# Four-head attention: the target row of a batch's first source tile added by a TensorE identity product instead of by VectorE

## The chip, the core and the metric

One NeuronCore of one Trainium2 chip runs the whole program; the other cores are idle. The metric is the device time of one execution in microseconds. The core has five engines that work through their own instruction lists in order and wait for each other on semaphores: TensorE (PE in the profile; its weight loads are PEld), VectorE (DVE), ScalarE (ACT), GpSimd (POOL) and SyncE (SP), which here issues DMAs.

## The reference, cut to what matters

The program is a four-layer graph network over 3125 nodes with 256 features. The change touches one of its stages, the first attention of the last layer, with HEADS = 4 and HID = 64:

```python
h = (x @ W).reshape(n, heads, ch)
es = (h * a_src).sum(-1)
ed = (h * a_dst).sum(-1)
e = jax.nn.leaky_relu(es[src] + ed[dst], 0.2)
m = jax.ops.segment_max(e, dst, num_segments=n)
w = jnp.exp(e - m[dst])
den = jax.ops.segment_sum(w, dst, num_segments=n)
alpha = w / den[dst]
out = jax.ops.segment_sum(h[src] * alpha[:, :, None], dst, num_segments=n)
```

The kernel computes it densely: for every head, every source node s and every target node t it forms the weight exp(leaky_relu(es[s] + ed[t]) - m[t]), multiplies it by the number of edges from s to t, and sums over the sources with matmuls.

## The kernel before

The stage is `dense_attention(K, "att2", given, 4, LOOPED, ...)`. The 3125 nodes are 25 tiles of 125 (`NPT`). A round `r` is one head `h = r // 5` and one group `g = r % 5` of five target tiles (`GW` = 625 targets in the free dimension); there are 20 rounds. A round has five batches (`q` = 0 to 4) of five source tiles (`UN` = 5), so there are 100 batches `b`. A batch lives in one of four ring slots, `ring[:, b % RB]`, as 125 source partitions x 5 tiles x 625 targets in fp32. The leaky ReLU is split: with `src8` = 0.8 es, `src2` = 0.2 es and `dst8` = 0.8 ed, the exponent is relu(src8 + dst8[t]) + low[t] + src2, where low[t] = 0.2 ed[t] - m[t]. The rows dst8 and low, the same in all 128 partitions, are `rows[:, r % 2, 0, :]` and `rows[:, r % 2, 1, :]` (the target row).

Each batch passes through these steps, each an instruction list's part on its engine:

- ACT `bend(b)` (L2009): five Relu activations of the dst8 row with bias src8 into the ring, semaphore `s_z`. It is issued two batches ahead, and waits for TensorE to have finished batch b-4 of the slot.
- DVE `lower(b)` (L1915): one tensor_tensor of 3125 columns adds the target row to all five tiles, semaphore `s_w` (in batch 0, five instructions of one tile).
- ACT exps (L2051): five Exp activations with bias src2, in place, semaphore `s_e`; they wait for `s_w`.
- DVE `weigh(b)` (L1934): min with 1 and times the edge counts `cell`, 3125 columns, semaphore `s_p`; it waits for all five exps.
- PE, for each of the five tiles, two accumulating matmuls (L2113 with 500 and L2115 with 125 columns; each shows as two instructions, since fp32 takes two passes) into PSUM banks 0 and 1 or 2 and 3, semaphore `s_mm`.

DVE's order is `lower(b+1)`, `weigh(b)`, then as a rule one `look` (L1875, 3125 columns of masks, the maximum for a coming round; the 100 looks are done by batch 92), and in q = 2 also `shift` (L1885 to L1890, five-column steps). ACT's order in batch b is: exps of b; in q = 3 `rows_out(r+1)` (L1990, L1991: the new rows from PSUM banks 5, 6 and 7); in q = 1 of the groups 1, 2 and 3 of the first three heads `row_out` (L1997: up to three copies of the next head's source scores, out of banks 5, 6 and 7); `bend(b+2)`; in q = 1 `evict(r-1)` (L2020, L2022: the finished sums to SBUF); in q = 2 `settle(r-1)` (L2034, L2035). PE's order in batch b is: the matmuls of b; in q = 0 `turn_back(r-1)` (L2095, waits for `evict`); in q = 2 `spread(r+1)` (L2078, 20 instructions that write banks 5, 6 and 7, after `shift`); in q = 4 of the first three groups of the first three heads `row` (L2085, up to 24 instructions that write banks 5, 6 and 7). SP loads the cells and masks into three buffers each. In the last head DVE also does `finish` in q = 3 (L1942 to L1948).

The same function with one head (att1 and att3, `fused`) has other steps, which the change leaves as they are.

Of the kernel before, what the change touches and what calls it, by code (L numbers as in the profile page):

```python
# [6 lines left out]
ALU = mybir.AluOpType  # L7
ACT = mybir.ActivationFunctionType
# [8 lines left out]
P = 128  # L17
# [3 lines left out]
NPT = 125  # L21
# [10 lines left out]
UN = 5  # L32
GW = UN * NPT
# [1757 lines left out]
def dense_attention(K, tag, given, heads, loops, bias_name, relu=False, to_aux=False):  # L1791
# [4 lines left out]
    f, NG5 = D // heads, NT // UN  # L1796
    NGR = heads * NG5
# [6 lines left out]
    MM, OUTS = (2, 2) if across else (UN, 2 * UN)  # L1804

# [4 lines left out]
    with Phase(nc, tag) as ph:  # L1810
# [6 lines left out]
        if across:  # L1817
            s_turned, s_back, turned = ph.sem("turned"), ph.sem("back"), ph.sb("turned", [P, GW])
        rows = ph.sb("rows", [P, 2, 2, GW])
# [46 lines left out]
        def _(dve):  # L1866
# [26 lines left out]
            def lower(b):  # L1893
# [3 lines left out]
                parts = UN if b == 0 else 1  # L1897
# [13 lines left out]
                for i in range(0 if fused else parts):  # L1911
                    n = UN // parts
                    dve.wait_ge(s_z, b * UN + (i + 1) * n)
                    here = ring[0:NPT, b % RB, i * n:(i + 1) * n, :]
                    dve.tensor_tensor(here, here, rows[0:NPT, r % 2, 1, :].unsqueeze(1).to_broadcast([NPT, n, GW]),  # L1915
                                      ALU.add).then_inc(s_w, n)
# [39 lines left out]

            dve.tensor_scalar(dst8[0:NPT, :, 0:heads], K.score_dst[0:NPT, :, 0:heads], 0.8, None, ALU.mult).then_inc(s_parts, 1)
# [25 lines left out]
        def _(act):  # L1983

            def rows_out(r):

                act.wait_ge(s_wide, r + 1)
                if r >= 2:
                    act.wait_ge(s_w, (r - 1) * UN * UN)
                act.copy(rows[:, r % 2, :, 0:BAND], K.ps[:, 5:7, 0:BAND]).then_inc(s_rows, 1)  # L1990
                act.copy(rows[:, r % 2, :, BAND:GW], K.ps[:, 7, 0:2 * NPT].rearrange("p (j n) -> p j n", j=2)).then_inc(s_rows, 1)  # L1991
# [7 lines left out]
            def bend(b):  # L1999

                r = b // UN
                h = r // NG5
                if b % UN == 0:
                    act.wait_ge(s_rows, (r + 1) * 2)
                for u in range(UN):
                    s = b % UN * UN + u
                    if b >= RB:
                        act.wait_ge(s_mm, ((b - RB) * UN + u + 1) * MM)
                    act.activation(ring[0:NPT, b % RB, u, :], rows[0:NPT, r % 2, 0, :], ACT.Relu,  # L2009
                                   bias=src8[0:NPT, s, h:h + 1]).then_inc(s_z, 1)  # L2010
# [34 lines left out]
            for b in range(NB):  # L2045
                r, q = b // UN, b % UN
                h, g = r // NG5, r % NG5
                for u in range(UN):
                    act.wait_ge(s_w, b * UN + (u + 1 if fused or b == 0 else UN))
                    here = ring[0:NPT, b % RB, u, :]  # L2050
                    act.activation(here, here, ACT.Exp, bias=src2[0:NPT, q * UN + u, h:h + 1]).then_inc(s_e, 1)  # L2051
                if q == 3 and r + 1 < NGR:
                    rows_out(r + 1)
                if q == 1 and g in (1, 2, 3) and h + 1 < heads:
                    for j in range(3 if g < 3 else 1):
                        row_out(h + 1, (g - 1) * 3 + j, 5 + j)
# [11 lines left out]
        def _(pe):  # L2068
# [28 lines left out]

            for i in range(7):
                row(0, i, i)
            pe.wait_ge(s_rowed, 7)  # L2100
            pe.wait_ge(s_parts, 3)
            spread(0)
            for b in range(NB):
                r, q = b // UN, b % UN
                h, g = r // NG5, r % NG5
                for v in range(UN):
# [18 lines left out]
                if q == 2 and r + 1 < NGR:  # L2125
                    spread(r + 1)
                if q == 4 and g < 3 and h + 1 < heads:
                    pe.wait_ge(s_rows, (r + 2) * 2)
                    for j in range(3 if g < 2 else 1):
                        row(h + 1, g * 3 + j, 5 + j)  # L2130
# [970 lines left out]
```

## Time and profile before

| what | value |
|---|---|
| median of 3 runs | 6654.85 us (6648.68 to 6659.43) |
| profiled execution, its own time | 6659.23 us |
| span of the profile | 6657.5 us |
| granted TensorE clock, mean over the span | 0.896 |
| four-head attention in the profile | from 4942.8 to 6018 us |

All times are microseconds unless ns is written. DVE, ACT and PE are busy when an instruction of theirs runs. An idle time in square brackets is that before the instruction, with what released it. The granted clock is a share of 2.4 GHz; it has the two levels 2.4 and 1.2 GHz.

### The profile page before, as it was taken

What the parts mean: (1) busy time and instruction counts of PE and PEld (TensorE: products, weight loads), DVE (VectorE), ACT (ScalarE), POOL (GpSimd) and SP (SyncE); (2) the same over time, 40 slices, a digit from 0 to 9 for tenths busy, and PEclk for the clock granted to TensorE, in tenths of its full rate; (3) what the DMA queues carried; (4) which work ended last, traced back from release to release, by engine and by line L of the source; (5) the groups of instructions that cost most, each with busy time, mean ns of one, the idle gap of its engine ahead of it and who ended that gap; (6) DMA issues with size and microseconds to landing.
All of it is one profiled execution on the core that took longest, in us unless ns stands there. A gap on an engine that the chain in (4) does not pass through costs nothing. (4 is left out here: it accounts for less than half of the span.)

```text
span 6657.5 us, 73453 instructions
## 1 busy us (share of the span) xinstructions
PE 4892.2 (73%) x21195; PEld 3419.5 (51%) x21196; DVE 4365.2 (66%) x7225; ACT 2060.1 (31%) x3736; POOL 1498.1 (23%) x1522
## 2 busy tenths in 40 slices
PE   0110888877888899999697789399927777776989
PEld 0000444433444677788585658378823333334877
DVE  9991999858999433423794370301049999997956
ACT  0000111131111233322332233122227777773432
POOL 4776666515666000011000010200020000000010
PEclk9995899978999899999898989599968888887989
DMA  3330333473334200044330012256534444433310
GB/s 96 139 128 24 102 100 101 93 305 114 113 100 98 44 9 15 7 114 118 117 115 28 2 47 75 93 181 183 166 96 157 153 156 153 155 127 98 127 33 20
DMA packets 376014, 682.91 MB, mean 103 GB/s; under 512 B 90858, under 2 KB 302883, under 8 KB 368132
## 3 DMA queue, kind: packets, MB, share of 16 engines
q1 hardware_dynamic: 300148, 522.74, 24.0%
q0 software_dynamic: 75344, 157.40, 9.2%
q8 instruction: 87, 1.43, 0.1%
q14 instruction: 115, 0.94, 0.0%
q10 hardware_dynamic: 320, 0.40, 0.0%
HBM read 507.64 MB, written 172.62 MB: 102 GB/s over the span
## 5 line engine op out<-in xcount | busy, mean ns | idle before, releaser
L896 PE MATMUL ps<-sum_hot_cell,sum_hot_src 128*128 128x500 bf16 x2640 | 762.1, 391 | 363.9 <-DVE sum_hot_src L835 221.2
L813 POOL DMA_INDIRECT sum_rows_in<-rel_table,rel_row x880 | 835.0, 949 | 471.5 <-issue 235.6
L837 DVE TENSOR_SCALAR sum_hot_cell<-x_nodes 128x1500 bf16<-128x1500 f16 (+1 forms) x880 | 892.0, 1014 | 2.2 <-issue 2.2
L2113 PE MATMUL ps<-att_ring,acc 125*65 125x500 f32 x1000 | 603.0, 689 | 306.8 <-DVE att_ring L1934 306.8
L2051 ACT ACTIVATE att_ring<-att_ring,att_src 125x625 f32<-125x625 f32 x750 | 555.8, 808 | 257.1 <-DVE att_ring L1909 158.1
L902 PE MATMUL ps<-sum_rows_in,sum_hot 128*128 128x256 f32 x1760 | 582.2, 411 | 50.0 <-issue 48.2
L896 PEld LDWEIGHTS ps<-sum_hot_cell,sum_hot_src 128*128 128x128 bf16 x2640 | 265.2, 101 | 668.8 <-issue 480.8
L2121 PE MATMUL ps<-acc,att_ring 125*125 125x257 f32 x2500 | 556.1, 385 | 45.9 <-DVE att_ring L1934 45.9
L2121 PEld LDWEIGHTS ps<-acc,att_ring 125*125 125x125 f32 x2500 | 474.6, 190 | 124.6 <-DVE att_ring L1934 50.3
L1875 DVE CUSTOM_DVE_ANT_0 att_held<-att_held,aux 125x3125 bf16<-125x3125 bf16 x150 | 510.3, 3408 | 33.2 <-ACT aux L1997 21.1
L1934 DVE SCALAR_TENSOR_TENSOR att_ring<-att_ring,att_held 125x3125 f32<-125x3125 f32 (+1 forms) x162 | 511.7, 3165 | 1.6 <-ACT att_ring L2051 1.3
L669 POOL DMA_INDIRECT rec_dram<-rec,addr x392 | 429.4, 1095 | 124.0 <-issue 124.0
L902 PEld LDWEIGHTS ps<-sum_rows_in,sum_hot 128*128 128x128 f32 x1760 | 314.2, 199 | 183.9 <-issue 91.1
L857 ACT COPY acc<-ps 128x256 f32<-128x256 f32 x50 | 18.6, 372 | 1143.5 <-PE ps L902 790.3
L2744 POOL TENSOR_TENSOR x_nodes<-x_nodes,aux 128x256 f32<-128x256 f32 x25 | 20.3, 852 | 1561.0 <-POOLq L118 1561.0
L833 DVE TENSOR_SCALAR sum_hot<-row_f,slot_dst,slot_w 128x128 f32<-128x128 f32 x880 | 308.6, 351 | 93.3 <-remote 47.9
L2009 ACT ACTIVATE att_ring<-att_rows,att_src 125x625 f32<-125x625 f32 x500 | 363.3, 803 | 0.6
L1915 DVE TENSOR_TENSOR att_ring<-att_ring,att_rows 125x3125 f32<-125x3125 f32 (+1 forms) x104 | 341.2, 3284 | 12.0 <-ACT att_ring L2009 11.9
L2115 PEld LDWEIGHTS ps<-att_ring,acc 125*65 125x65 f32 x1000 | 155.8, 156 | 353.4 <-issue 353.4
L1662 DVE TENSOR_TENSOR experts_y<-ps,expert_bo 128x256 f32<-128x256 f32 x200 | 84.9, 424 | 362.1 <-PE ps L1729 362.1
L1048 PE MATMUL ps<-aux,sum_wide 125*125 125x256 f32 x1250 | 298.5, 386 | 14.0 <-ACT sum_wide L986 14.0
L2113 PEld LDWEIGHTS ps<-att_ring,acc 125*65 125x65 f32 x1000 | 137.1, 158 | 326.3 <-DVE att_ring L1934 326.3
(471 smaller groups left out, 8347.5 us busy)
## 6 DMA issues: line engine op xcount, KB each, us to landing
att_held<-cells SPq DMA_DIRECT2D x150, 781.2 KB, 4.7
att_held<-masks SPq DMA_DIRECT2D x150, 762.9 KB
rel_table<-rel_stage SPq DMA_DIRECT2D x50, 2048.0 KB, 6.5
ffn_w<-in_L_ffn_W SPq DMA_DIRECT2D x64, 1024.0 KB, 7.6
sum_cell<-cells SPq DMA_DIRECT2D x125, 156.2 KB, 4.6
sage_cell<-cells SPq DMA_DIRECT2D x125, 156.2 KB, 2.2
masks<-att_held POOLq DMA_DIRECT2D x25, 762.9 KB, 11.8
sum_rows_in<-rel_table,rel_row POOLq DMA_INDIRECT x880
```

The source lines that it names most:

```text
L669: pool.indirect_dma_start(K.rec_dram, bass.IndirectOffsetOnAxis(addr[:, j:j + 1], 0), rec[:, j, :], None).then_inc(scattered[j % 2], 16)
L813: pool.indirect_dma_start(rows_in[:, b, u, :], None, table, bass.IndirectOffsetOnAxis(rows[:, k:k + 1], 0)).then_inc(gathered[b], 16)
L837: dve.tensor_scalar(hot_cell[:, b, u, :], K.columns[:, :, 0:CW], K.cell[:, k], None, ALU.is_equal).then_inc(s_hot, 1)
L896: pe.matmul(K.ps[:, bass.ds(side * 4 + j, 1), 0:BW].rearrange("p a n -> p (a n)"), hot_src[:, b, u, :], hot_cell[:, b, u, j * BW:(j + 1) * ...
L902: pe.matmul(K.ps[:, bass.ds(side * 4 + 3, 1), 0:D].rearrange("p a n -> p (a n)"), hot[:, b, u, :], rows_in[:, b, u, :], start=False, stop= ...
L1875: dve.tensor_tensor_reduce(out=masks[0:NPT, n % MB, 0:N], in0=masks[0:NPT, n % MB, 0:N], in1=srow[h][0:NPT, :], scale=1.0, scalar=-BIG, op ...
L1915: dve.tensor_tensor(here, here, rows[0:NPT, r % 2, 1, :].unsqueeze(1).to_broadcast([NPT, n, GW]), ALU.add).then_inc(s_w, n)
L1934: dve.scalar_tensor_tensor(out=here, in0=here, scalar=1.0, in1=cell[0:NPT, b % CB3, i * n * GW:(i + 1) * n * GW], op0=ALU.min, op1=ALU.mul ...
L2009: act.activation(ring[0:NPT, b % RB, u, :], rows[0:NPT, r % 2, 0, :], ACT.Relu, bias=src8[0:NPT, s, h:h + 1]).then_inc(s_z, 1)
L2051: act.activation(here, here, ACT.Exp, bias=src2[0:NPT, q * UN + u, h:h + 1]).then_inc(s_e, 1)
L2113: pe.matmul(K.ps[0:W, side, 0:BAND], node_rows[s][0:NPT, h, :], ring[0:NPT, b % RB, v, 0:BAND], start=s == 0, stop=s == NT - 1).then_inc(s ...
L2121: pe.matmul(K.ps[0:NPT, u, 0:W], ring[0:NPT, b % RB, v, u * NPT:(u + 1) * NPT], node_rows[s][0:NPT, h, :], start=s == 0, stop=s == NT - 1) ...
```

## The change

For the four-head stage `LIFT` = 1 and `MINE` = 4: DVE's `lower` handles the tiles 1 to 4 of a batch (2500 columns). For tile 0, PE computes one identity product with a row of ones, in two matmuls of 512 and 113 columns: `lift_w` is 126 x 125, the identity with a last row of ones, and the moving operand is ring partitions 0 to 125, where partition 125 holds the target row. The result, tile plus target row, lies in PSUM banks 6 and 7 (`lifted`), and the first exp of a batch reads it from there. ACT writes the target row into partitions 96 to 127 of the ring's tile 0 before the first Relu of a batch (a copy of 625 columns), in the batches q = 0 to 3, which are the four slots, and waits for its own copy.

`lift(b+1)` stands on PE ahead of the matmuls of b. It waits for the first Relu of b+1 and for the first exp of b; in q = 4 also for `rows_out(r+1)`, and in q = 1 of the rounds with `row_out` also for those copies, as banks 6 and 7 are shared. `spread` and `row` wait for the first exp of the next batch for the same reason. `row_out` moves from q = 1 to q = 0.

```diff
+    LIFT = 1 if across else 0
+    MINE = UN - LIFT
...
+            lift_w, last = ph.sb("lift_w", [P, NPT]), ph.sb("last", [P, 1])
+            KL = NPT + 1
+            lifted = K.ps[:, 6:8, :].rearrange("p a n -> p (a n)")[0:NPT, 0:GW]
...
-                for i in range(0 if fused else parts):
-                    n = UN // parts
-                    dve.wait_ge(s_z, b * UN + (i + 1) * n)
-                    here = ring[0:NPT, b % RB, i * n:(i + 1) * n, :]
+                for i in range(0 if fused else MINE if b == 0 else 1):
+                    n = 1 if b == 0 else MINE
+                    dve.wait_ge(s_z, b * UN + LIFT + (i + 1) * n)
+                    here = ring[0:NPT, b % RB, LIFT + i * n:LIFT + (i + 1) * n, :]
...
+            if across:
+                link(dve.tensor_scalar(last[:, :], K.col_f[:, :], float(NPT), None, ALU.is_equal))
+                dve.tensor_scalar(lift_w[:, :], K.ident[:, 0:NPT], last[:, 0:1], None, ALU.add).then_inc(s_lift_w, 1)
...
+                    if u == 0 and b % UN < RB:
+                        act.copy(ring[96:P, b % RB, 0, :], rows[96:P, r % 2, 1, :]).then_inc(s_lift_w, 1)
+                        act.wait_ge(s_lift_w, 2 + r * RB + b % UN)
...
-                    act.wait_ge(s_w, b * UN + (u + 1 if fused or b == 0 else UN))
                     here = ring[0:NPT, b % RB, u, :]
-                    act.activation(here, here, ACT.Exp, bias=src2[0:NPT, q * UN + u, h:h + 1]).then_inc(s_e, 1)
+                    if u < LIFT:
+                        act.wait_ge(s_lift, b + 1)
+                    else:
+                        act.wait_ge(s_w, b * MINE + (u - LIFT + 1 if fused or b == 0 else MINE))
+                    act.activation(here, lifted if u < LIFT else here, ACT.Exp,
+                                   bias=src2[0:NPT, q * UN + u, h:h + 1]).then_inc(s_e, 1)
...
-                if q == 1 and g in (1, 2, 3) and h + 1 < heads:
+                if q == (0 if across else 1) and g in (1, 2, 3) and h + 1 < heads:
...
+            def lift(b):
+
+                pe.wait_ge(s_z, b * UN + 1)
+                if b > 0:
+                    pe.wait_ge(s_e, (b - 1) * UN + 1)
+                r, q = b // UN, b % UN
+                h, g = r // NG5, r % NG5
+                if q == 4 and r + 1 < NGR:
+                    pe.wait_ge(s_rows, (r + 2) * 2)
+                if q == 1 and g in (1, 2, 3) and h + 1 < heads:
+                    pe.wait_ge(s_rowed, (h + 1) * 7 + min(g * 3, 7))
+                for x, y in ((0, 512), (512, GW)):
+                    mm = pe.matmul(K.ps[0:NPT, 6 + x // 512, 0:y - x], lift_w[0:KL, :], ring[0:KL, b % RB, 0, x:y], start=True, stop=True)
+                mm.then_inc(s_lift, 1)
...
             for b in range(NB):
...
+                if across and b + 1 < NB:
+                    lift(b + 1)
...
                 if q == 2 and r + 1 < NGR:
+                    if across:
+                        pe.wait_ge(s_e, (b + 1) * UN + 1)
                     spread(r + 1)
                 if q == 4 and g < 3 and h + 1 < heads:
                     pe.wait_ge(s_rows, (r + 2) * 2)
+                    if across:
+                        pe.wait_ge(s_e, (b + 1) * UN + 1)
```

## Rows read from the trace of the kernel before

**Rows 1.** The page's head and its first part.

```profile
span 6657.5 us, 73453 instructions
PE 4892.2 (73%) x21195; PEld 3419.5 (51%) x21196; DVE 4365.2 (66%) x7225; ACT 2060.1 (31%) x3736; POOL 1498.1 (23%) x1522
```

**Rows 2.** Busy time by window: the four-head attention (window, length, engines, clock, DMA share, GB/s).

```profile
4942.80:6018.00 1075.20, 739.92 (x2700) 365.49 (x2700) 1038.97 (x551) 774.30 (x1150) 0.00 (x0) 0.85 0.44 143
```

**Rows 3.** Groups by form in that window (count, busy us, mean ns, idle before).

```profile
L2051 ACT ACTIVATE att_ring<-att_ring,att_src 125x625 f32<-125x625 f32 x500 | 363.7, 804 | 99.0 <-DVE att_ring L1915 99.0
...
L1915 DVE TENSOR_TENSOR att_ring<-att_ring,att_rows 125x3125 f32<-125x3125 f32 x99 | 337.6, 3410 | 4.5 <-ACT att_ring L2009 4.4
```

**Rows 4.** The longest wait of ACT, 4980 to 5950 us (total, times, longest).

```profile
ACT att_rows L1990 <- PE ps L2078: 147.3, 18, 10.0
```

**Rows 5.** Timeline, start of the stage (start us, us, engine, line, shape, count).

```profile
4978.82 7.17 ACT L2009 ACTIVATE att_ring<-att_rows,att_src 125x625 f32<-125x625 f32 x10
4980.12 3.69 DVE L1915 TENSOR_TENSOR att_ring<-att_ring,att_rows 125x625 f32<-125x625 f32 x5 [7.50 <-ACT att_ring L2009]
4983.72 1.08 DVE L1921 TENSOR_TENSOR att_held<-att_held,ident 125x125 uint16<-125x125 uint16 x5
```

**Rows 6.** Groups by form over the whole span, ACT.

```profile
L986 ACT CAST sum_wide<-sum_cell 128x625 f32<-128x625 uint16 x125 | 84.6, 712 | 196.5 <-DMA sum_cell<-cells 136.6 <-PE ps L1048 54.6 <-ACTq L980 5.2
L2826 ACT ACTIVATE ffn_h<-ps,ffn_b 128x320 f32<-128x320 f32 x80 | 42.2, 527 | 116.4 <-PE ps L2853 116.3
```

**Rows 7.** Timeline of a round's end: q = 2 to q = 4.

```profile
5428.42 3.41 DVE L1934 SCALAR_TENSOR_TENSOR att_ring<-att_ring,att_held 125x3125 f32<-125x3125 f32 x1
5431.74 3.41 DVE L1875 CUSTOM_DVE_ANT_0 att_held<-att_held,aux 125x3125 bf16<-125x3125 bf16 x1
5431.88 1.05 PE L2113 MATMUL ps<-att_ring,acc 125*65 125x500 f32 x2 [1.59 <-DVE att_ring L1934]
5437.21 1.28 PE L2078 MATMUL ps<-ident,att_dst 125*128 125x125 f32 x10
5439.64 0.99 ACT L1990 COPY att_rows<-ps 128x1000 f32<-128x1000 f32 x1 [7.46 <-PE ps L2078]
5440.94 3.65 ACT L2009 ACTIVATE att_ring<-att_rows,att_src 125x625 f32<-125x625 f32 x5
5444.49 3.63 ACT L2051 ACTIVATE att_ring<-att_ring,att_src 125x625 f32<-125x625 f32 x5
5445.86 3.41 DVE L1915 TENSOR_TENSOR att_ring<-att_ring,att_rows 125x3125 f32<-125x3125 f32 x1
5449.19 3.41 DVE L1934 SCALAR_TENSOR_TENSOR att_ring<-att_ring,att_held 125x3125 f32<-125x3125 f32 x1
```

**Rows 8.** Timeline, the handover of the next head's scores.

```profile
5102.58 2.84 PE L2085 MATMUL ps<-ident,score 125*128 125x125 f32 x24
5104.33 3.41 DVE L1875 CUSTOM_DVE_ANT_0 att_held<-att_held,aux 125x3125 bf16<-125x3125 bf16 x1
5104.93 1.49 ACT L1997 COPY aux<-ps 128x500 f32<-128x500 f32 x3
5105.26 1.00 PE L2113 MATMUL ps<-att_ring,acc 125*65 125x500 f32 x2
```

**Rows 9.** Timeline, eviction, and a batch's first matmuls after a long idle time.

```profile
5415.82 0.56 ACT L2020 COPY att_turned<-ps 65x500 f32<-65x500 f32 x1
5417.24 0.66 PE L2095 MATMUL ps<-ident,att_turned 65*125 65x65 f32 x5
5421.90 1.93 PE L2113 MATMUL ps<-att_ring,acc 125*65 125x500 f32 x2 [4.00 <-DVE att_ring L1934]
```

**Rows 10.** Busy time by window: granted clock is the third from the end.

```profile
5401.90:5405.30 3.40, 3.36 (x6) 1.41 (x7) 3.40 (x3) 3.40 (x6) 0.00 (x0) 0.50 0.68 198
5411.90:5417.40 5.50, 5.48 (x22) 2.65 (x23) 5.50 (x3) 4.64 (x9) 0.00 (x0) 1.00 0.61 178
```

**Rows 11.** Busy time by window: the batches without a look.

```profile
5963.40:5992.00 28.60, 23.24 (x80) 10.41 (x78) 27.82 (x10) 28.60 (x43) 0.00 (x0) 0.88 0.35 109
```

More of the change, by code:

```diff
@@ L1818, in dense_attention @@
             s_turned, s_back, turned = ph.sem("turned"), ph.sem("back"), ph.sb("turned", [P, GW])
+            s_lift, s_lift_w = ph.sem("lift"), ph.sem("lift_w")
+            lift_w, last = ph.sb("lift_w", [P, NPT]), ph.sb("last", [P, 1])
+            KL = NPT + 1
+            lifted = K.ps[:, 6:8, :].rearrange("p a n -> p (a n)")[0:NPT, 0:GW]
         rows = ph.sb("rows", [P, 2, 2, GW])
@@ L1896, in lower @@
                 h = r // NG5
-                parts = UN if b == 0 else 1
                 if b % UN == 0:
@@ L1988, in rows_out @@
                 if r >= 2:
-                    act.wait_ge(s_w, (r - 1) * UN * UN)
+                    act.wait_ge(s_w, (r - 1) * UN * MINE)
                 act.copy(rows[:, r % 2, :, 0:BAND], K.ps[:, 5:7, 0:BAND]).then_inc(s_rows, 1)
@@ L2102, in _ @@
             spread(0)
+            if across:
+                pe.wait_ge(s_lift_w, 1)
+                lift(0)
             for b in range(NB):
@@ L2128, in _ @@
                     pe.wait_ge(s_rows, (r + 2) * 2)
+                    if across:
+                        pe.wait_ge(s_e, (b + 1) * UN + 1)
                     for j in range(3 if g < 2 else 1):
```

## The prediction

> **What bounds the kernel now.** The change touches only the four-head attention, so I read that stage. The page's first part [rows 1] gives shares of the whole span and decides nothing. The busy time of the stage's window [rows 2] does: in 1075.2 us DVE is busy 1039, ACT 774 and PE 740, at a granted clock of 0.85. The groups by form [rows 3] show that DVE hardly waits: 4.4 us before 99 `lower` instructions, against 99 us that the exps wait for DVE. So DVE sets the pace, with three instructions of 3125 columns a batch. One counts as 3.33 us on the path, the distance from 5445.86 to 5449.19 in the timeline [rows 7]; the shown 3.41 overlaps the next instruction.
>
> The cover is thin in one place. ACT's longest waits are for `spread` [rows 4], and what follows nearly meets DVE [rows 7]: the new rows are copied from 5439.64, the Relus of the next round's first batch run from 5440.94, the exps of q = 4 from 5444.49 to about 5448.07, and the `weigh` that needs them starts at 5449.19. That is 1.1 us of slack once a round.
>
> **What it saves.** Five `lower` instructions of one tile take 3.69 us [rows 5], so one advances by (3.69 - 0.80) / 4 = 0.72. From 625 to 3125 columns the advance grows from 0.72 to 3.33, or 0.652 a tile; the fixed part stays. In the last eight batches, without looks, ACT is busy 28.6 of 28.6 us [rows 11], so there a shorter `lower` saves nothing. 92 x 0.652 = 60.0 us saved.
>
> **What it adds on ACT.** Eighty copies of 625 columns. The nearest row is a copy of 625 columns from SBUF to SBUF at 0.712 us [rows 6]; with the wait for itself I take 0.76 (0.05 is about the distance from a releaser's end to the next start [rows 7]). Bounds: 0.56, the time of a 500-column copy [rows 9], and 0.95, an activation of 0.80 [rows 3] with a slow wait. An average batch costs ACT 774 / 100 = 7.7 us, then 8.3, while DVE needs 9.3 + 0.2, so on average it is hidden; in the chains below it isn't. The first exp reads PSUM. An activation with bias from PSUM takes 0.527 for 320 columns [rows 6]; 305 more at 0.86 ns (copies from PSUM: 1000 columns 0.99 [rows 7], 500 columns 0.56 [rows 9]) give 0.79 against the 0.80 of rows 3, taken as no change; bounds -0.1 and +0.1.
>
> The Trainium skill (VectorE: DVE Perf Modes, "The TRN2 errata") has ScalarE pay 52 cycles less, about 0.04 us, for a PSUM source; an estimate by it takes at most 2 us off this sum, since a chain below holds one such exp; the rows above bear out 0.01.
>
> **What it adds on PE.** `lift` streams 512 + 113 = 625 columns, as many as one tile's matmuls: five tiles take 5437.21 - 5431.88 = 5.33 at full clock, so 1.06 us; at the lower level twice that, as two 500-column instructions take 1.93 instead of 1.05 [rows 9, 7]. Together 106 to 213 us on an engine with 335 idle us. The two DVE instructions for `lift_w` at the start stand where DVE waits for the first masks anyway: nothing. No DMA moves; SP's loads are asked for 0.65 us a batch earlier at a DMA share of 0.44 [rows 2]: nothing.
>
> **Chain 1, once in each of 19 rounds.** Let T be the end of q = 2's `weigh`, 5431.74 [rows 7]. Before: rows copied from T+7.9, Relus until T+12.75, exps of q = 4 until T+16.4, `lower` of the next batch at T+14.1, `weigh` of q = 4 at T+17.45. After, DVE is two tiles quicker and wants that `weigh` at T+16.15. `lift(q4)` starts when the rows are out (T+9.2) and is hidden. But the copy pushes the Relus to T+13.5 and the exps to T+17.1. So DVE waits 0.95 us: 19 x 0.95 = 18.1 us given back.
>
> **Chain 2, in the nine handover rounds** (groups 1 to 3 of three heads). PE's `row` follows the matmuls of q = 4, and `row_out` moves to q = 0, so ACT now waits for PE where it used to find finished scores, and `lift(q1)` waits for `row_out`. Let T0 be the end of q = 4's `weigh`. In the terms of chain 1 PE's matmuls of q = 3 and the next `lift` end by T+16.6 and T0 is T+20.4, so PE has idled 3.9 us. After 4.00 idle us the first two 500-column instructions took 1.93, after 1.59 they took 1.05 [rows 9, 7]; the clock reads 0.50 in such a stretch, the level of 1.2 GHz, and 1.00 in the other [rows 10]. I take 8.0 us for the five tiles (5.3 at full clock). `row` takes 2.84 [rows 8], so T0+10.9; the last score copy ends at T0+11.4, the ones-row copy and five Relus at T0+15.8. DVE wants them for `lower(q2)` at 3.33 + 2.68 + 3.33 + 3.33 = T0+12.7: it waits 3.1 (2.0 in group 1, where the self-loops add 1.08 [rows 5]). The exps of q = 1 then end at T0+19.4, 0.9 after DVE wants them. ACT does copy and Relus of q = 3 and `evict` until T0+24.5 (about 0.8 for its two copies, 0.56 for the first [rows 9]), `turn_back` takes 0.66 [rows 9], and `lift(q2)`, which stands behind it on PE, ends at T0+26.3; the exps of q = 2 end at T0+30.0, while DVE wants them at 28.75: 1.3. Together 4.2, 5.3, and in group 3, with one source tile to hand over, 2.7; 12.2 a head, 36.6 us for three.
>
> PE keeps its order here: DVE is past the `weigh` at 5104.33, but the batch's matmuls begin at 5105.26, behind the 24 instructions of `row` [rows 8]. The Trainium skill (TensorE: Matmul & The Clock Gate, "Step-by-step: what each phase is for") has matmuls stay in program order, only weight loads being pulled ahead; by that rule, the trace agrees, the 1.3 us are due. If `lift` could pass `turn_back` the sum would be 12 us lower.
>
> **Ends.** At the start two copies stand before the first two batches (1.5) and `lower(0)` is shorter (0.65): +0.8. In the last eight batches ACT has four more copies (3.0), and `turn_back` and `lift` stand between `evict` and the next exps once (1.9): +4.9.
>
> **Sum.** -60.0 + 18.1 + 36.6 + 0.8 + 4.9 = +0.4 us. The profiled execution's span of 6657.5 would become 6658; its own time, 6659.23, is 4.4 above the median, so I forecast 6655 for the median of 6654.85: a measurement of this kernel can tell about 0.2%, 13.3 us, from no change.
>
> **Rivals.**
> A. DVE keeps the pace alone, because the chains have more slack than read: -60 + 5.7, so 6600. For it: DVE is 97% busy, ACT 72%. Against: 1.1 us of slack in rows 7, of which 1.3 are asked. 0.06.
> B. PE stays at full clock at the handover, since `lift` breaks its pauses: the tiles of q = 4 take 5.3 instead of 8.0, which takes 2.7 off the six rounds with full handover and 0.5 off the others, and a further 0.9 where `weigh(q1)` then meets its time: some 22 us less, 6633. For it: pauses of 1.6 us kept the clock [rows 7]. Against: the pause at that place is near 4. 0.15.
> C. Slower: PE's clock falls in q = 2. Then `spread` comes 2.7 us later, and chain 1 has no slack left to take it: every such round costs 2.7 more. It decides when PE's pause ahead of q = 2's matmuls nears 4 us, where 1.6 are shown [rows 7] and `lift` and a late `turn_back` should shorten it. In ten of 19 rounds +27: 6682. Costly copies or a slow wait of ACT for itself (+0.2 in each of 28 chain passages twice: +11) push the same way. 0.16.
> D. It doesn't do what it says: the four-tile `lower` is no shorter than 3.33. Then the chains' waits shrink by as much as DVE is later, and what stays is ends and handover, about 6675. Rows 5 speak against it. 0.03.
> Forecast case: 0.60.
>
> **Numbers.** Bounds: low, B with the cheap copy and exp, -22; high, C in part, with the dear copy, +15. Range 6633 to 6670, which leaves out A and the far end of C and D. Faster by over 0.2%: A, B without its edge, and a corner of the forecast: 0.21. Slower by over 0.2%: C, D: 0.18. Within: 0.61.
>
> **What would show it.** `lower` at about 2.75 us, 99 of them. DVE's waits for ACT's Relus and exps, 4.4 us for the Relus before [rows 3], grow to 55 us or so. Rounds without handover take 48 to 50 us from `weigh` to `weigh`, below the 15 x 3.33 = 50 of three full instructions a batch, those with it 52 to 55. ACT's copies near 0.71. `lift` near 1.06 a batch, granted clock above 0.85. Wrong if DVE waits under 30 us (A), if the matmuls of q = 4 in handover rounds take 5.3 (B), or if those of q = 2 take 8 (C).

## The result and the profile after

| what | before | after |
|---|---|---|
| median of 20 runs each | 6656.59 us (6648.68 to 6664.47) | 6668.53 us (6658.27 to 6676.56) |
| ratio | | 1.0016, 95% interval 1.0009 to 1.0023 |
| profiled execution, its own time | 6659.23 us | 6664.07 us |
| four-head attention in that profile | 1075.0 us | 1084.6 us |

The change costs 12 us, 0.16% by the ratio: it lies within the 0.2% named in the prediction, and on the slow side of zero. The length of the stage, here and below, runs from the issue of the stage's bias load to the end of the last instruction that adds the bias. In this pair of profiles the rest of the program differed by 4.8 us the other way; nothing there was changed.

The stage by window (length, then busy us with counts of PE, PEld, DVE, ACT, POOL, granted clock, DMA share, GB/s), to be held against [rows 2]:

```profile
4943.60:6028.20 1084.60, 830.07 (x3100) 427.15 (x3100) 978.67 (x552) 833.78 (x1230) 0.00 (x0) 0.88 0.43 142
```

DVE is busy 60 us less, and the stage is 10 us longer. So DVE now waits some 70 us more, and no engine is full. The groups by form name for whom; the second and third answer to [rows 3]:

```profile
L1939 DVE SCALAR_TENSOR_TENSOR att_ring<-att_ring,att_held 125x3125 f32<-125x3125 f32 x99 | 337.5, 3409 | 49.7 <-ACT att_ring L2065 49.7
L1920 DVE TENSOR_TENSOR att_ring<-att_ring,att_rows 125x2500 f32<-125x2500 f32 x99 | 273.2, 2760 | 25.8 <-ACT att_ring L2020 25.7
L2065 ACT ACTIVATE att_ring<-ps,att_src 125x625 f32<-125x625 f32 x100 | 77.1, 771 | 78.1 <-PE ps L2125 78.1
L2018 ACT COPY att_ring<-att_rows 32x625 f32<-32x625 f32 x80 | 56.7, 709 | 2.1
L2110 PE MATMUL ps<-ident,att_turned 65*125 65x65 f32 x100 | 22.0, 373 | 81.1 <-ACT att_turned L2033 81.1
```

In these lines L1920 is `lower`, L1939 `weigh`, L2065 the exps, L2018 the new copies, L2125 `lift`, L2110 `turn_back`, L2033 the second copy of `evict`. `lower` fell from 3410 to 2760 ns, as wanted. What came instead is a chain across three engines: DVE waits 49.7 us for exps, the exps from PSUM wait 78.1 us for `lift`, and on PE `turn_back` waits 81.1 us for `evict`. The last of these is the surprise. The waits of PE and ACT one by one (total, times, longest):

```profile
PE ps L2110 <- ACT att_turned L2033: 81.1, 19, 6.3
ACT att_ring L2065 <- PE ps L2125: 78.1, 31, 5.1
DVE att_ring L1939 <- ACT att_ring L2065: 49.7, 36, 5.0
DVE att_ring L1920 <- ACT att_ring L2020: 34.2, 26, 8.5
```

19 times, once a round, PE stands in front of `turn_back`, 4.3 us on average, with `lift(q2)` behind it in its list. Before the change the same matmuls waited 1.5 us in all, three times. The timeline of one such passage, as [rows 9] have it of before:

```profile
5430.20 3.64 ACT L2020 ACTIVATE att_ring<-att_rows,att_src 125x625 f32<-125x625 f32 x5
5433.75 0.55 ACT L2031 COPY att_turned<-ps 65x500 f32<-65x500 f32 x1
5434.20 0.26 ACT L2033 COPY att_turned<-ps 65x125 f32<-65x125 f32 x1
5434.51 1.31 PE L2110 MATMUL ps<-ident,att_turned 65*125 65x65 f32 x5 [5.87 <-ACT att_turned L2033]
5435.62 2.41 PE L2125 MATMUL ps<-att_ring,att_lift_w 126*125 126x512 f32 x4
5436.23 2.76 DVE L1920 TENSOR_TENSOR att_ring<-att_ring,att_rows 125x2500 f32<-125x2500 f32 x1
5438.07 0.78 ACT L2065 ACTIVATE att_ring<-ps,att_src 125x625 f32<-125x625 f32 x1 [3.61 <-PE ps L2125]
5438.75 2.92 ACT L2065 ACTIVATE att_ring<-att_ring,att_src 125x625 f32<-125x625 f32 x4
5441.80 3.42 DVE L1939 SCALAR_TENSOR_TENSOR att_ring<-att_ring,att_held 125x3125 f32<-125x3125 f32 x1 [2.82 <-ACT att_ring L2065]
```

Read it downwards: the Relus end at 5433.8, `evict` at 5434.46, `turn_back` runs at half clock (1.31 us where [rows 9] have 0.66), `lift` too (2.41; at full clock the same record shows 1.3), the first exp starts 3.61 us after ACT was free, and DVE waits 2.82 us.

The Trainium skill has matmuls stay in program order, only weight loads being pulled ahead (TensorE: Matmul & The Clock Gate, "Step-by-step: what each phase is for"). By that rule `lift` can't pass `turn_back`, whose input alone is late; the trace agrees: by 5428.7 all that `lift` itself needs was there (the first Relu of its batch is over by 5423.1, the exp before it, which frees the banks, by 5426.6, the tiles of q = 0 by 5428.7), and it starts at 5435.62, behind `turn_back`.

Where the 9.7 us lie, taken from one `weigh` of q = 0 to the next in both timelines:

| part | before | after | change | predicted |
|---|---|---|---|---|
| start, to the first such `weigh` | | | +1.0 | -0.5 |
| round 0 | 60.3 | 59.2 | -1.1 | -2.3 |
| nine rounds with handover | 457.7 | 483.0 | +25.3 | +15.8 |
| nine rounds without | 467.3 | 445.5 | -21.8 | -17.5 |
| from round 19's to the end | 43.0 | 49.3 | +6.3 | +4.9 |

The last column spreads the forecast over the parts: 0.652 for each of the 92 `lower` instructions where they stand (two before the first such `weigh`, none in round 18), 0.95 for each chain 1, 36.6 for the handover rounds, and the two ends.

### The profile page after: what moved, and what is told of

It reads as the page before. It is cut to its first block and busy times, and to the rows that moved or that the text cites. A ratio compares the mean times of both kernels' runs of the same rounds, so it can differ in the third digit from the quotient of the medians.

```text
span 6662.4 us, 74445 instructions
## 1 busy us (share of the span) xinstructions
PE 4975.6 (75%) x21595; PEld 3477.7 (52%) x21596; DVE 4306.2 (65%) x7226; ACT 2119.3 (32%) x3816; POOL 1503.9 (23%) x1522
## 5 line engine op out<-in xcount | busy, mean ns | idle before, releaser
L2148 PE MATMUL ps<-att_ring,acc 125*65 125x500 f32 x1000 | 561.8, 646 | 104.7 <-DVE att_ring L1939 104.1
L1939 DVE SCALAR_TENSOR_TENSOR att_ring<-att_ring,att_held 125x3125 f32<-125x3125 f32 (+1 forms) x162 | 512.1, 3167 | 49.7 <-ACT att_ring L2065 49.7
L2156 PEld LDWEIGHTS ps<-acc,att_ring 125*125 125x125 f32 x2500 | 476.2, 191 | 122.5 <-DVE att_ring L1939 47.5
L2065 ACT ACTIVATE att_ring<-att_ring,att_src 125x625 f32<-125x625 f32 x650 | 484.2, 809 | 154.6 <-DVE att_ring L1914 154.6
L1881 DVE CUSTOM_DVE_ANT_0 att_held<-att_held,aux 125x3125 bf16<-125x3125 bf16 x150 | 510.5, 3409 | 31.1 <-ACT aux L2005 19.1
L2150 PEld LDWEIGHTS ps<-att_ring,acc 125*65 125x65 f32 x1000 | 148.5, 149 | 325.2 <-issue 325.2
L1920 DVE TENSOR_TENSOR att_ring<-att_ring,att_rows 125x2500 f32<-125x2500 f32 (+1 forms) x103 | 276.2, 2684 | 34.3 <-ACT att_ring L2020 34.2
L750 PE MATMUL ps<-ident,rel_xin 128*128 128x128 f32 x50 | 17.2, 448 | 353.1 <-DVE rel_xin L689 311.6
## 6 DMA issues: line engine op xcount, KB each, us to landing
masks<-att_held POOLq DMA_DIRECT2D x25, 762.9 KB, 11.9
```

What stands on the lines that cost most here:

```text
L1881: dve.tensor_tensor_reduce(out=masks[0:NPT, n % MB, 0:N], in0=masks[0:NPT, n % MB, 0:N], in1=srow[h][0:NPT, :], scale=1.0, scalar=-BIG, op ...
L1939: dve.scalar_tensor_tensor(out=here, in0=here, scalar=1.0, in1=cell[0:NPT, b % CB3, i * n * GW:(i + 1) * n * GW], op0=ALU.min, op1=ALU.mul ...
L2065: act.activation(here, lifted if u < LIFT else here, ACT.Exp, bias=src2[0:NPT, q * UN + u, h:h + 1]).then_inc(s_e, 1)
L2148: pe.matmul(K.ps[0:W, side, 0:BAND], node_rows[s][0:NPT, h, :], ring[0:NPT, b % RB, v, 0:BAND], start=s == 0, stop=s == NT - 1).then_inc(s ...
L2156: pe.matmul(K.ps[0:NPT, u, 0:W], ring[0:NPT, b % RB, v, u * NPT:(u + 1) * NPT], node_rows[s][0:NPT, h, :], start=s == 0, stop=s == NT - 1) ...
```

## The experiments

All ran on three other chips, on which the program as a whole takes 114 to 120 us less. So each is compared by its ratio to runs of the kernel before on its own chip, and by the length of the stage in its one profile. The changed kernel's stage was profiled again on one of the three: 1080.8 us, against 1084.6 in the first profile, so a few us between two stages say nothing. The kernel before has no stage profile there. Waits are DVE's for the Relus and for the exps, all of the stage, with some 8 us at its start that every version has.

| kernel | ratio to before (95%) | stage us | DVE waits, Relus + exps |
|---|---|---|---|
| changed_again | 1.0008 (0.9998 to 1.0018) | 1080.8 | 32.2 + 49.3 |
| drop_only | 0.9939 (0.9923 to 0.9956) | 1029.5 | 21.0 + 12.0 |
| drop_copy | 0.9947 (0.9930 to 0.9964) | 1064.8, of it 19.1 waits for edge counts | 31.2 + 14.7 |
| no_handover | 0.9960 (0.9941 to 0.9978) | 1039.3 | 23.3 + 18.5 |
| turn_late | 0.9970 (0.9960 to 0.9979) | 1058.0, of it 5.8 waits for edge counts | 33.8 + 19.5 |
| warm | 1.0010 (1.0001 to 1.0020) | 1085.8 | 42.9 + 43.3 |
| row_product | 1.0106 (1.0089 to 1.0123) | 1141.8 | 48.8 + 90.7 |
| row_dma | 0.9952 (0.9936 to 0.9969) | 1051.0 | 19.2 + 33.3 |
| row_dma_late | 0.9926 (0.9910 to 0.9943) | 1026.9 | 15.4 + 14.4 |
| copy_twice | 1.0068 (1.0051 to 1.0085) | 1129.1 | 59.0 + 69.9 |

### The change again

> The changed kernel once more, unaltered, beside the three other kernels of this call, so that all are compared with the same kernel before on one chip. Both theories: the stage at 1078 to 1088 us again, the ratio to before 1.001 to 1.002.

The repeat gives the base line, 1080.8 us, and the same pattern: nine handover rounds of 52 to 55 us, the others but the first 47 to 51.

### The saving alone

The kernel before with the four-tile `lower`; nothing adds the target row to tile 0, and its first exp waits for the Relu only.

```diff
-                for i in range(0 if fused else parts):
-                    n = UN // parts
+                for i in range(0 if fused else MINE if b == 0 else 1):
+                    n = 1 if b == 0 else MINE
...
+                    elif u == 0:
+                        act.wait_ge(s_z, b * UN + 1)
```

> The kernel before, with DVE's lower over tiles 1 to 4 only; tile 0 gets no target row and its exp waits for its Relu instead, so the output of the stage is not the reference's. No lift, no copy, row_out and turn_back as before. Chains theory (the gain is real and is given back by chains of ACT and PE): the stage falls from 1075 us to 1030 to 1046, some 30 to 45 of the 60 us, with small waits at chain 1 that remain even so. Rival, the shorter lower is worth little (another engine or a transfer takes its place at once): stage above 1065.

1029.5 us, and 47.5 us (0.61%) less than before by the medians. Of 60 us that `lower` gives, some 20 go into waits: 12.0 for exps (1.3 before), 18 of them, none over 1.4 us, and 21.0 for Relus (11.9 before):

```profile
DVE att_ring L1915 <- ACT att_ring L2009: 21.0, 11, 8.2
DVE att_ring L1934 <- ACT att_ring L2056: 12.0, 18, 1.4
```

It disposes of rival A: even with nothing added, DVE doesn't keep the pace alone. But the timeline, round by round, shows two sizes of this wait. In six rounds in which the matmuls of q = 2 ran at full clock (5.5 us from the first start to the last end) DVE waited 0.27 us before the `weigh` of q = 4 and no more: that is chain 1 with the 0.2 that its slack of 1.1 leaves without a copy. In nine others those matmuls took 7.0 to 8.5 us, `spread` came later, and the `weigh` of q = 4 and the `lower` of the next round waited 0.9 to 3.1 us together; 17.6 of the 19.2 us at these two places lie there. So most of what this kernel gives back is rival C's mechanism, the low clock in q = 2, and not the slack.

### Without the handover

The maxima of the later heads are taken from head 0's scores, so that no `row` and no `row_out` is needed after the first head, and `lift(q1)` has no `row_out` to wait for; the rest of the work is the same.

```diff
-                if q == 4 and g < 3 and h + 1 < heads:
+                if False:
...
-                if q == (0 if across else 1) and g in (1, 2, 3) and h + 1 < heads:
+                if False:
...
-                if q == 1 and g in (1, 2, 3) and h + 1 < heads:
-                    pe.wait_ge(s_rowed, (h + 1) * 7 + min(g * 3, 7))
```

> The changed kernel with row and row_out left out for the heads 1 to 3; the looks of all heads use head 0's source row, so the stage's maxima and its output are not the reference's; everything else runs as before. Chains theory: the nine handover rounds (483 us in the changed kernel) fall to the length of the others, 49.4, so the stage loses 38 to 45 us: 1040 to 1047. Rival, the sharing of banks costs nothing and the copies or lift do: less than 12 us gained.

All rounds but the first and the last three fall to 48.5 to 50.2 us, and the stage to 1039.3. So 41.5 us of the changed kernel's stage are bound to the handover, which itself is at most 24 short matmul instructions and three copies a round. The ratios put it at 0.48%, 31 us, with about 13 us to either side. DVE's waits at the three places of chain 2 (`weigh(q1)`, `lower(q2)`, `weigh(q2)`) are 42.0 us in the nine rounds of the repeat and 0 here. The predicted price of chain 2, 36.6, was of the right size. Which part of it comes from moving `row_out` to q = 0 and which from the sharing of banks 6 and 7, no run tells.

### turn_back one batch later

```diff
-                if across and q == 0 and r > 0:
+                if across and q == 1 and r > 0:
                     turn_back(r - 1)
```

> The changed kernel, with turn_back(r-1) after the matmuls of q = 1 instead of q = 0, so that lift(q2) no longer stands behind the wait for evict. Chains theory: of the 75 us that DVE waits in the changed kernel 30 stand before weigh of q = 2; they go, and the stage falls from 1084.5 us to about 1055 to 1062, with turn_back's waits (81 us on PE) near zero and the first exp's waits for lift near 20. Rival, PE's clock or ACT's load alone sets the pace: the waits move to q = 3 or q = 4 and the stage stays above 1078.

One line takes 22.8 us off the stage; by the ratios it is 0.38%, 25 us. In the profiled execution two waits for edge counts, 4.8 and 1.0 us, stand as well, which the repeat of the changed kernel does not have; without them it would be 28.6. The same passage, timeline of this kernel:

```profile
4950.18 0.55 ACT L2031 COPY att_turned<-ps 65x500 f32<-65x500 f32 x1
4950.64 0.26 ACT L2033 COPY att_turned<-ps 65x125 f32<-65x125 f32 x1
4950.79 0.78 ACT L2065 ACTIVATE att_ring<-ps,att_src 125x625 f32<-125x625 f32 x1
4955.34 3.41 DVE L1939 SCALAR_TENSOR_TENSOR att_ring<-att_ring,att_held 125x3125 f32<-125x3125 f32 x1
4957.29 0.66 PE L2110 MATMUL ps<-ident,att_turned 65*125 65x65 f32 x5
```

The exp follows `evict` at once, since `lift(q2)` was done during PE's idle time, the `weigh` of q = 2 waits for nothing, and `turn_back` takes 0.66 us behind matmuls that kept the clock up. Over the stage the waits before q = 2's `weigh` fell from 30.4 to 1.4 us.

### A warm PE in front of turn_back

Is it the order on PE or the low clock that costs? Ten short products into unused columns run while PE would wait for `evict`, the order stays.

```diff
-                pe.wait_ge(s_turned, (r + 1) * 2)
...
+                if r < NGR - 1:
+                    for k in range(10):
+                        pe.matmul(K.ps[0:NPT, 4, UN * W:512], lift_w[0:NPT, :],
+                                  K.ident[0:NPT, 0:1].to_broadcast([NPT, 512 - UN * W]), start=True, stop=True)
+                pe.wait_ge(s_turned, (r + 1) * 2)
```

> The changed kernel, with ten idle products (187 columns each, about 3 us at full clock) into unused columns of bank 4 ahead of turn_back's wait for evict; their result is never read. It tells the wait itself from the clock that falls during it. If the low clock is what made the wait before weigh of q = 2 3 us a handover round instead of the 1.3 that I had: turn_back and lift(q2) take 0.66 and 1.1 to 1.3 instead of 1.3 and 2.4, those waits fall by some 10 to 15 of 30 us, and the stage to 1068 to 1078, less what PE's added work costs where evict is early. Rival, only the order of the wait counts: the stage stays at 1082 to 1090, since PE is busier and no sooner.

`turn_back` got quicker, 309 ns a piece instead of 373, and PE's wait for `evict` fell from 81 to 28 us, yet the stage grew by 5 us:

```profile
L2113 PE MATMUL ps<-ident,att_turned 65*125 65x65 f32 x100 | 17.1, 309 | 28.2 <-ACT att_turned L2033 28.1
```

The waits before q = 2's `weigh` fell by 6.2 us (30.4 to 24.2), those before `lower` of q = 0 rose by 8.5 (7.2 to 15.7). Both come from the clock. The products end some 3 us before `evict` does, and only in three of the nine handover rounds did `turn_back` still find full clock (0.76 us for its five). This is one of them:

```profile
5262.32 0.76 PE L2113 MATMUL ps<-ident,att_turned 65*125 65x65 f32 x5 [3.06 <-ACT att_turned L2033]
5262.91 1.48 PE L2128 MATMUL ps<-att_ring,att_lift_w 126*125 126x512 f32 x4
5268.16 3.42 DVE L1939 SCALAR_TENSOR_TENSOR att_ring<-att_ring,att_held 125x3125 f32<-125x3125 f32 x1 [1.37 <-ACT att_ring L2065]
```

DVE waits 1.37 us here and 1.29 in the round before, where the changed kernel has 2.82 in both: the 1.3 of the prediction. In the third `lift` took 2.16 and DVE waited 2.06; in the other six the clock was down for some or all of `turn_back` and the wait is 2.5 to 2.8. So of the 2.8 us the order on PE accounts for 1.3 and the low clock for the other 1.5, and the other order takes all of it. What the products cost is seen in rounds 5, 9, 10, 15 and 18: there the matmuls of q = 2 took 7.2 us instead of the 5.5 of the repeat, `spread` came later, and the `lower` after it waited 1.7 us more each time, 8.5 in all. Why the clock fell there is not shown.

### Copies without lift

`drop_only` with ACT's 80 copies.

```diff
+                    if u == 0 and b % UN < RB:
+                        act.copy(ring[96:P, b % RB, 0, :], rows[96:P, r % 2, 1, :]).then_inc(s_lift_w, 1)
+                        act.wait_ge(s_lift_w, 1 + r * RB + b % UN)
```

> As the kernel before with the four-tile lower alone (tile 0 without its target row), plus ACT's 80 copies of the target row and its wait for each of them; no lift. Chains theory: in the former run DVE waited 1.4 us at most before a weigh, so nearly every copy in chain 1 and some more come through: the stage goes from 1029.5 to 1045 to 1055. Rival, ACT has room for the copies (772 busy of 1029 us): under 1035.

The stage of the profiled run was 1064.8 us, above what was expected, but three waits for edge counts stand in it that belong to no theory:

```profile
DVE att_held L1922 <- DMA att_held<-cells: 19.1, 3, 7.1
DVE att_ring L1916 <- ACT att_ring L2013: 31.2, 19, 9.0
DVE att_ring L1935 <- ACT att_ring L2060: 14.7, 18, 1.4
```

Without them it is 1045.7. The ratios put it 0.08% above `drop_only`, 5 us, each with an interval of 0.17%, 11 us, to either side. The totals say that the copies cost something without a `lift`, and not how much. The rounds do: where the matmuls of q = 2 ran at full clock, chain 1's two waits are 0.93 us (0.77 and 0.16) where `drop_only` has 0.27, and where they took 7.2, 2.6 us where it has 1.9. A copy on chain 1 costs 0.7 us a round, as forecast (0.76).

### No copy, the row by a second product

The identity product takes 125 partitions, and a product of one partition, ones by the target row, adds to it in PSUM.

```diff
-                    mm = pe.matmul(..., lift_w[0:KL, :], ring[0:KL, b % RB, 0, x:y], start=True, stop=True)
+                    pe.matmul(..., K.ident[0:NPT, 0:NPT], ring[0:NPT, b % RB, 0, x:y], start=True, stop=False)
+                    mm = pe.matmul(..., K.ones[0:1, 0:NPT], rows[0:1, r % 2, 1, x:y], start=False, stop=True)
```

> The changed kernel without ACT's 80 copies: the target row comes in by a second accumulating product, a row of ones from one partition times one partition of the rows tile, so lift takes twice the columns on PE (2.1 us a batch instead of 1.06). The output is the reference's. Chains theory: each passage of a chain is 0.76 us shorter on ACT, 20 us over chain 1 and 9 to 15 at the handover, less what the longer lift adds behind turn_back (some 9): stage 1045 to 1062. Rival, PE is what is short (busy 829 of 1078 us): it gets slower, above 1090.

A miss, and a large one: 61 us longer than with copies. The product of one row costs as much PE time as one of 125, and the four together take longer than their columns. Timeline at full clock (weight loads are PEld):

```profile
5418.50 1.02 PE L2122 MATMUL ps<-att_ring,ident 125*125 125x512 f32 x2
5419.45 0.29 PEld L2123 LDWEIGHTS ps<-att_rows,ones 1*125 1x125 f32 x2 [0.76 <-issue]
5419.45 1.12 PE L2123 MATMUL ps<-att_rows,ones 1*125 1x512 f32 x2
5420.50 0.47 PE L2122 MATMUL ps<-att_ring,ident 125*125 125x113 f32 x2
5420.90 0.47 PE L2123 MATMUL ps<-att_rows,ones 1*125 1x113 f32 x2
5421.40 0.78 ACT L2062 ACTIVATE att_ring<-ps,att_src 125x625 f32<-125x625 f32 x1 [3.08 <-PE ps L2123]
```

The four products take 5421.30 - 5418.50 = 2.80 us, where twice the `lift` of the changed kernel, 1.06, would be 2.12. PE is busy 1029 of 1142 us, and 76 of the 100 batches' first exps wait for it (215.8 us in all). PE, which had 250 idle us, was no free place to put the copies' work.

### The row by DMA

SP brings the target row, 2.5 KB, into partition 125 of a slot's first tile; `lift` waits for it, ACT copies nothing. First together with the late `turn_back`:

```diff
+            def row_in(b):
+                if across and b % UN < RB:
+                    r = b // UN
+                    sp.wait_ge(s_rows, (r + 1) * 2)
+                    if b >= RB:
+                        sp.wait_ge(s_lift, b - RB + 1)
+                    sp.dma_start(ring[NPT:NPT + 1, b % RB, 0, :], rows[NPT:NPT + 1, r % 2, 1, :]).then_inc(s_in[b % RB], 16)
```

> The changed kernel with two of the causes taken away: turn_back after the matmuls of q = 1, and the target row brought into ring partition 125 by a DMA from SP's queue (80 of 2.5 KB) in place of ACT's 80 copies. The output is the reference's. Chains theory: from the 1058.0 of the run with the late turn_back alone, 19 times 0.76 for chain 1 and about as much in handover rounds go: 1030 to 1042, ratio to before 0.992 to 0.996. Rival, the DMAs land too late for lift, or the sequence of PE takes over as with the doubled lift: above 1055.

1026.9 us, 3 below the expected range (the ratio, 0.9926, lies in its own): as short as `drop_only`, which leaves the row out altogether, and 0.74% quicker than before (0.57 to 0.90). The stage by window:

```profile
4827.00:5853.90 1026.90, 787.57 (x3100) 405.83 (x3100) 976.22 (x552) 771.81 (x1150) 0.00 (x0) 0.93 0.46 150
```

And DVE's two waits, of which 7.9 us stand at the start:

```profile
DVE att_ring L1937 <- ACT att_ring L2034: 15.4, 8, 7.9
DVE att_ring L1956 <- ACT att_ring L2079: 14.4, 24, 1.4
```

The DMA part alone:

> The changed kernel with turn_back where it stands (q = 0), but without ACT's 80 copies: SP brings the target row by DMA into partition 125 of the slot's first tile (2.5 KB each, asked for when the rows are out and the slot's lift of four batches before is done), and lift waits for that DMA. It differs from row_dma_late in turn_back's place alone, and from the changed kernel in the copies alone. Theory (copies and turn_back's place cost separately; the copies lie on both chains, 19 rounds with one on the way and nine with two, plus four in the last batches: 19 x 0.76 + 9 x 1.5 + 3 = 31 us): stage 1050 to 1060 us. Rival 1 (the copies only hurt because turn_back blocks PE behind them): stage below 1040. Rival 2 (the early turn_back alone is what costs, the copies nothing): above 1070.

1051.0 us. With the row by DMA the stage is 29.8 us shorter, with the late `turn_back` 22.8, with both 53.9: the two costs add up, to within the few us by which two profiles differ (52.6, or 58.4 without the 5.8 us of waits for edge counts in `turn_late`), and neither rival holds. The sum of the theory, 31, is nearer than its parts: of the 29.8, 24.4 lie in the nine handover rounds, where it had 20, and only 1.2 in the nine others, where it had 7, since in two of them the matmuls of q = 2 took 7.2 us instead of 5.5. And 12.9 of the 29.8 came off the wait before `weigh(q2)`, behind `turn_back`, so there is some truth in the first rival. `lift` itself, the 100 products that the change is named for, costs the stage nothing net once these two are gone: `row_dma_late`, with it, is as short as `drop_only`, without it. What it costs by itself isn't measured, because the two also differ in how often the matmuls of q = 2 ran slow (five rounds with it, ten without).

### Each copy twice

```diff
+                        act.wait_ge(s_lift_w, 2 + 2 * (r * RB + b % UN))
+                        act.copy(ring[96:P, b % RB, 0, :], rows[96:P, r % 2, 1, :]).then_inc(s_lift_w, 1)
+                        act.wait_ge(s_lift_w, 3 + 2 * (r * RB + b % UN))
```

> The changed kernel with each of ACT's 80 copies made twice, each waited for; same output. Theory (a copy delays the set end only on the two chains and at the two ends, 19 x 0.76 + 9 x 1.5 + 3 = 31 us for 61 us of added work of ACT): stage 28 to 42 us longer than the 1080.8 of the repeat of the changed kernel, so 1109 to 1123. Rival 1 (ACT has room, 833 of 1085 us busy, and the copies are hidden): under 10 us longer. Rival 2 (ACT sets the pace everywhere): 55 us or more longer.

48.3 us longer: above the theory (28 to 42), which missed here, and below the rival that ACT sets the pace everywhere (55 or more). By the stages the first set of copies costs 29.8 of the 60 us that they occupy ACT, the second 48.3; by the ratios to before it is 0.56% and 0.60%, 37 and 39 us, each with about 13 us to either side. So the times don't settle whether the second set is dearer. The timeline shows where it would be: six of the nine rounds without handover grew by 3 us (from 48.7 and 49.5 to 51.7 and 52.4), because in them q = 2's `weigh` now waits 2.0 to 2.2 us for its exps, where with one copy it did not wait at all. There the first copy used up slack that the second would have needed.

## Why the prediction came out as it did

The predicted time was 6655 and the measured one 6668.5, in the range, within 0.2% of before. The cancelling of saving and costs was right in kind. One term was too low by 13.7 us, and the range held only because two others, the first half of chain 2 and chain 1, were too high by 6.8 and 3.2: without these the time would lie near 6678, outside. That part is luck. By the parts of the table above, the 9.3 us between forecast (+0.4) and measured stage (+9.7) are +1.5 at the start, +1.2 in round 0, +9.5 in the handover rounds, -4.3 in the nine others, and +1.4 at the end.

**Right: the saving.** `lower` takes 2760 ns, 0.65 less, for 99 instances. 60.0 us were counted, and DVE is busy 60.3 us less. (The sum takes `lower(0)` twice, in the 92 and again at the start, 0.65 us.) That a shorter `lower` saves nothing in the last eight batches held: round 18 fell by 0.4 us.

**Right in mechanism, a little too dear: chain 1.** 18.1 us were predicted, 0.95 in each of 19 rounds. DVE waited 10.2 us before the `weigh` of q = 4, 0.73 in each of 14 rounds, and 7.8 before `lower` of q = 0, of which 3.1 stood there before the change: 14.9 net. Rounds 16 and 17, where DVE also does `finish`, have no such wait. In the nine rounds without handover the two waits grew by 4.7 us where 8.6 were forecast, which is most of the -4.3 above. The timeline shows it as worked out, `rows_out`, copy, Relus, exps, and DVE late by 0.16 and 0.73 us:

```profile
5401.05 0.99 ACT L1998 COPY att_rows<-ps 128x1000 f32<-128x1000 f32 x1 [3.95 <-PE ps L2093]
5402.35 0.71 ACT L2018 COPY att_ring<-att_rows 32x625 f32<-32x625 f32 x1
5403.09 3.64 ACT L2020 ACTIVATE att_ring<-att_rows,att_src 125x625 f32<-125x625 f32 x5
5406.87 2.77 DVE L1920 TENSOR_TENSOR att_ring<-att_ring,att_rows 125x2500 f32<-125x2500 f32 x1 [0.16 <-ACT att_ring L2020]
5410.36 3.42 DVE L1939 SCALAR_TENSOR_TENSOR att_ring<-att_ring,att_held 125x3125 f32<-125x3125 f32 x1 [0.73 <-ACT att_ring L2065]
```

**Right in kind, the first half of chain 2.** `row` follows the matmuls of q = 4 and ACT waits for it:

```profile
5043.52 1.93 PE L2148 MATMUL ps<-att_ring,acc 125*65 125x500 f32 x2 [3.72 <-DVE att_ring L1939]
...
5051.86 2.84 PE L2100 MATMUL ps<-ident,score 125*128 125x125 f32 x24
5052.96 0.58 ACT L2005 COPY aux<-ps 128x500 f32<-128x500 f32 x1 [5.13 <-PE ps L2100]
...
5059.83 2.76 DVE L1920 TENSOR_TENSOR att_ring<-att_ring,att_rows 125x2500 f32<-125x2500 f32 x1 [2.71 <-ACT att_ring L2020]
```

From 5043.52 to `row` at 5051.86 the five tiles took 8.3 us (8.0 forecast), after an idle time of 3.72 (3.9 forecast), and `lower(q2)` waited 2.71 (this is a group 1, where 2.0 were forecast). But this is the slowest of nine such passages. With the same idle time of 3.7 ahead of them, the others took 8.15 once, 7.0 six times and 5.3, full clock throughout, once. So the 8.0 was too high by 0.9 on average, and over nine rounds `lower(q2)` and `weigh(q1)` waited 12.4 + 5.7 = 18.1 us where the sum held 36.6 - 9 x 1.3 = 24.9.

**Mis-sized: the last term of chain 2.** "`turn_back` takes 0.66 [rows 9], and `lift(q2)`, which stands behind it on PE, ends at T0+26.3 ...: 1.3." The wait before `weigh(q2)` is 2.82 in the timeline and 25.4 in nine rounds, 13.7 more than 9 x 1.3. The step that failed: 0.66 and 1.06 are times at full clock. They come from a kernel in which PE hardly waited in front of `turn_back` (1.5 us in the stage). By the prediction's own times PE was idle there for 6.7 us (from `row_out` at T0+11.4, 1.06 of `lift` and 5.3 of q = 0's tiles later, to T0+24.5; measured in such a round: 6.26), and for the matmuls of q = 4 it had charged the low clock after 3.9. From the end of `evict` to the next exp it took 3.61 us instead of the 1.8 counted. The same omission is in the end's term: there the timeline shows 3.54 us where 1.9 were set, which makes +6.3 of +4.9. In the handover rounds +13.7 and the -6.8 of the first half make +6.9 of the +9.5; the other 2.6 are not accounted for. The run `warm` shows the same term at full clock: where `turn_back` and most of `lift` ran there, DVE waited 1.3 us, as predicted.

**Found by the runs, missed before.** That the order on PE is what makes this place dear was written down ("if `lift` could pass `turn_back` the sum would be 12 us lower"); `turn_late` measured 22.8. The run `warm` says that added products, the order kept, bring the clock up at `turn_back` in only three of the nine rounds, and gain nothing in the end. And DVE's waits for Relus and exps grew to 83.9 us, 75 without the start, where about 55 were named as the sign.

**The rivals.** A: DVE keeps pace alone: refuted by `drop_only`. B: full clock at the handover: refuted in eight of nine passages, true in one. C: low clock in q = 2: the five tiles took 5.5 us from first start to last end in 18 of 20 rounds, and 8.2 and 7.0 in the others (before: seven of 20 at 7.0 to 8.1); refuted for this kernel, though a low clock did push to the slow side, in another place. As a mechanism C is real: in `drop_only` it costs most of what is given back. D: refuted by 2760 ns.

**Other terms.** Copies 709 ns (0.712 taken). The exps from PSUM took 771 ns, those from SBUF 806, 0.035 less, where the rows had led me to 0.01. The Trainium skill has ScalarE pay 52 cycles, about 0.04 us, less for a PSUM source (VectorE: DVE Perf Modes, "The TRN2 errata"); here the trace agrees with the page and not with my interpolation. On 100 exps that is 3.5 us of ACT, on the chains 2 at most.

## What to carry to other kernels

When work moves from the bound engine to others, walk their instruction lists in program order, and ask at every wait what stands behind it: a product that the bound engine needs must not be queued behind one that waits for a late, unimportant result. The move here paid nothing (+0.16%) with `turn_back` in front of `lift` and the row copied by ACT, and 0.74% with `turn_back` a batch later and the row brought by a DMA; the idea was sound, its placing was not. And when you cost a stretch after an idle time that the change itself creates, don't take its durations from rows without one: cost it at both levels of the clock, because after the same idle time both were seen here.

## What the runs showed of the hardware

- The same idle time of TensorE is followed by either level of the clock. In the changed kernel the five tiles of q = 4 came after 3.7 to 3.9 us of idle time in 17 rounds and took 5.5 us in two of them, 7.2 in ten and 8.2 to 8.5 in five (first start to last end). `turn_back` ran at full clock after 3.2 us (0.76 us, three rounds) and mostly at half after 2.47 (1.21 to 1.28, three rounds).
- Two accumulating products of 125 and of 1 partition into the same bank, 512 and 113 columns each, take 2.80 us for the four, against 2.12 for twice `lift`, whose products all have one shape; the weight load of the product of one partition starts with that product (5419.45 for both, 0.76 us "issue" ahead of it, against 0.24 in `lift`). Whether the number of partitions or the alternating weights cause this, the run doesn't separate. The product of one partition streams as long as that of 125 (1.12 and 1.02 us for 512 columns).
- A DMA of one partition's row of 2.5 KB, 80 of them on SP's queue among the big loads, was in time for all but one `lift` (one wait of 9.0 us at the stage's start).
- In the profiled executions of `drop_copy` and `turn_late` three and two loads of edge counts came late, by up to 7.1 and 4.8 us; nothing in the kernels explains it, and it stays open.
- Not tried: `lift` on PE in an order of its own per round (ahead of `row`), which would touch the rest of chain 2; `row_out` left in q = 1; and `warm` with fewer products.
